# Main probabilities of a windowed attention turned as 64-row halves on TensorE, lower and upper queries into one PSUM bank each

## The reference, cut to what matters

```python
def light_attn(x, ln_g, ln_b, w_qkv, w_out):
    xn = layernorm(x, ln_g, ln_b)
    q, k, v = jnp.split(xn @ w_qkv, 3, axis=-1)
    q, k, v = (towin(q), towin(k), towin(v))
    kk, vv = (around(k), around(v))
    sim = jnp.einsum('bhnwd,bhnWd->bhnwW', q * DH ** (-0.5), kk)
    sim = jnp.where(kmask[None, None, :, None, :], sim, -jnp.finfo(sim.dtype).max)
    attn = jax.nn.softmax(sim, axis=-1)
    o = jnp.einsum('bhnwW,bhnWd->bhnwd', attn, vv)
    return o.transpose(0, 2, 3, 1, 4).reshape(b, n, HDH) @ w_out
```

## Time and profile before

| what | value |
|---|---|
| median of 3 executions | 4277.84 us (4275.5 to 4278.29) |
| the profiled execution's own time | 4279.63 us |
| its span, first to last instruction | 4277.9 us |
| mean granted TensorE clock | 0.968 |
| TensorE matmul busy | 3981.5 us (93%) |
| TensorE weight loads busy | 3281.4 us (77%) |
| VectorE busy | 2822.5 us (66%) |
| ScalarE busy | 1786.3 us (42%) |
| GpSimd busy | 876.8 us (20%) |

### The profile page before, as it was taken

The page is one execution under the profiler, slowest core; times in us unless marked ns, Lnnn a source line. Parts: engine busy times, 40 slices in busy tenths (PEclk is TensorE's granted clock), DMA queues, the critical chain, the costliest instruction groups (busy, mean ns, idle before and its releaser), DMA issues. The chain is left out here.

```text
span 4277.9 us, 96936 instructions
## 1 busy us (share of the span) xinstructions
PE 3981.5 (93%) x39328; PEld 3281.4 (77%) x39328; DVE 2822.5 (66%) x5012; ACT 1786.3 (42%) x4746; POOL 876.8 (20%) x663
## 2 busy tenths in 40 slices
PE   6788779999999999989999999968999999999998
PEld 5677767888888888878888888857777677777776
DVE  9888857776767676665555567574745646646546
ACT  7434323444444344434444433332544544534434
POOL 0222202222222322222222222221111011111011
PEclk9899979999999999999999999987999999999999
DMA  9688852322222232212221212122022022122021
GB/s 318 168 227 220 225 163 72 92 86 83 85 92 83 83 94 82 86 57 63 60 61 60 60 60 61 54 88 60 7 55 58 9 55 48 19 53 51 16 45 14
DMA packets 341371, 360.91 MB, mean 84 GB/s; under 512 B 23104, under 2 KB 237376, under 8 KB 340928
## 3 DMA queue, kind: packets, MB, share of 16 engines
q1 hardware_dynamic: 262592, 287.52, 22.7%
q0 software_dynamic: 12288, 33.56, 3.8%
q10 hardware_dynamic: 66048, 33.56, 2.9%
HBM read 228.21 MB, written 76.02 MB: 71 GB/s over the span
## 5 line engine op out<-in xcount | busy, mean ns | idle before, releaser
L1684 POOL TENSOR_TENSOR l_prob<-l_prob,l_inv 128x768 f32<-128x768 f32 x256 | 389.8, 1544 | 1690.9 <-DVE l_inv L1641 1690.9
L1235 ACT ACTIVATE l_prob<-l_ps_s,l_neg_max 128x192 f32<-128x192 f32 x1024 | 420.7, 443 | 7.6 <-DVE l_neg_max L1617 7.4
L2244 ACT ACTIVATE h_prob<-h_ps_s,h_neg_max 128x1024 f32<-128x1024 f32 x256 | 285.6, 1116 | 253.6 <-DVE h_neg_max L2318 253.6
L1617 DVE TENSOR_REDUCE l_neg_max<-l_ps_s 128x4 f32<-128x768 f32 x256 | 233.1, 952 | 237.4 <-PE l_ps_s L1004 218.4
L2315 DVE TENSOR_REDUCE h_neg_max<-h_ps_s 128x1 f32<-128x1024 f32 x256 | 312.4, 1221 | 50.9 <-PE h_ps_s L2103 42.6
L2372 DVE COPY h_probs_t<-h_ps_t 128x512 f32<-128x512 f32 x256 | 176.5, 690 | 180.4 <-PE h_ps_t L2117 180.1
L2134 PEld LDWEIGHTS h_ps_o<-h_probs_t,ahead_then_values 128*64 128x64 f32 x4096 | 223.8, 138 | 45.4 <-issue 45.4
L2134 PE MATMUL h_ps_o<-h_probs_t,ahead_then_values 128*64 128x128 f32 x4096 | 254.9, 278 | 0.0
L2117 PEld LDWEIGHTS h_ps_t<-ident,h_prob 64*128 64x128 f32 x4096 | 151.6, 140 | 112.0 <-issue 66.2
L1235 ACT ACTIVATION_READ_ACCUMULATOR l_prob<-l_ps_s,l_neg_max 128x1 f32 x1024 | 235.5, 230 | 0.0
L1004 PEld LDWEIGHTS l_ps_s<-l_k_t,l_q_t 64*64 64x64 f32 x6144 | 187.9, 132 | 48.1 <-issue 44.8
(11 more groups left out here) (413 smaller groups left out, 10800.0 us busy)
## 6 DMA issues: line engine op xcount, KB each, us to landing
toep_back<-taps_padded ACTq DMA_DIRECT2D x32, 1024.0 KB, 11.1
x<-xg SPq DMA_DIRECT2D x64, 512.0 KB, 9.1
l_xin<-x SPq DMA_DIRECT2D x128, 256.0 KB, 3.3
l_xres<-x SPq DMA_DIRECT2D x128, 256.0 KB, 3.2
l_val_side<-l_val SPq DMA_DIRECT2D x256, 128.0 KB, 3.1
out_dram<-l_res SPq DMA_DIRECT2D x128, 256.0 KB, 2.0
ahead_then_values<-x SPq DMA_DIRECT2D x126, 256.0 KB, 3.1
xin<-in_L_attn_x_dram SPq DMA_DIRECT2D x32, 768.0 KB, 6.4
```

Of the source, the lines that this page charges most:

```text
L1235: last = nc.scalar.activation(prob[t % 2][:, h, pair, :], ps_s[:, h, pair, BOTH], ACT.Exp, bias=neg_max[:, t % 2, h, pair:pair + 1], accum ...
L1617: nc.vector.tensor_reduce(neg_max[:, t % 2, h, :], ps_s[:, h, :, BOTH], AX_X, ALU.max, negate=True).then_inc(max_made, 1)
L1684: nc.gpsimd.tensor_tensor(mine, mine, spread(inv[:, t % 2, h, :], [1, PAIRS], [0, WIN + P]), ALU.mult).then_inc(p_normed, 1)
L2244: nc.scalar.activation(prob[i % 2][:, :].rearrange("p (a k) -> p a k", a=2), ps_s[i % 2][:, :, :], ACT.Exp, bias=neg_max[:, qt % 2, h:h + ...
```

## The change

Each transpose of 128 queries by 128 keys becomes two of 64 queries by 128 keys, one in the lower and one in the upper 64 rows of the array. The lower 64 queries of all eight heads go to `ps_b`, the upper ones to `ps_a`, so that VectorE and ScalarE each copy one half of the queries of every head instead of all queries of one half of the heads. As both banks are now written from the first pair on, the waits for `u1_kept` and `u2_kept` stand ahead of `turn_side`.

```diff
-                def turn_main(bank, j, h, made):
-                    for pair in range(PAIRS):
-                        last = nc.tensor.transpose(bank[:, pair * P:(pair + 1) * P], prob[j % 2][:, h, pair, MAIN],
-                                                   ident[:, :])
-                    last.then_inc(made, 1)
+                def turn_main(j):
+
+                    for n in range(HEADS):
+                        for rows, bank, made in ((LO, ps_b, main0_made), (HI, ps_a, main1_made)):
+                            last = nc.tensor.transpose(bank[:, n * WIN:(n + 1) * WIN],
+                                                       prob[j % 2][rows, n // PAIRS, n % PAIRS, MAIN], ident[rows, rows])
+                            if n == HEADS - 1:
+                                last.then_inc(made, 1)
...
                         wait(pe, p_normed, 2 * (g - 7))
+                        wait(pe, u1_kept, done(g - 3))
+                        wait(pe, u2_kept, done(g - 2))
                         wait(pe, res_made, g - 9)
                         turn_side(t)
-                        wait(pe, u1_kept, done(g - 3))
-                        turn_main(ps_b, t, 0, main0_made)
-                        wait(pe, u2_kept, done(g - 2))
-                        turn_main(ps_a, t, 1, main1_made)
+                        turn_main(t)
...
-                        nc.scalar.activation(pt_main[:, 1, :, :].rearrange("p a q -> p (a q)"), ps_a[:, :],
+                        nc.scalar.activation(pt_main[:, :, :, HI], ps_a[:, :].rearrange("p (h a q) -> p h a q", h=2, q=WIN),
...
-                        nc.vector.tensor_copy(pt_main[:, 0, :, :].rearrange("p a q -> p (a q)"),
-                                              ps_b[:, :]).then_inc(main0_kept, 1)
+                        nc.vector.tensor_copy(pt_main[:, :, :, LO],
+                                              ps_b[:, :].rearrange("p (h a q) -> p h a q", h=2, q=WIN)).then_inc(main0_kept, 1)
```

## The result

The changed kernel takes 4295.04 us (median of 7 runs, 4292.45 to 4297.32) against 4277.84 us for the kernel before, run beside it (7 runs too): a ratio of 1.0033 with a 95% interval of 1.0021 to 1.0045. It is slower, by 0.33%. The forecast was 4286 us, with 4270 to 4300 as its range and "slower by over 0.2%" as the likeliest of the three. The profiled execution has a span of 4294.0 us against 4277.9, so 16.1 us are to be accounted for, where the prediction's sum had 7.9. The median, 9 us above the point forecast, lies in the stated range but outside the 4280 to 4293 that the prediction gave its likeliest case.

A forecast was written before the change was run, and what follows sets the result against it. The prediction took TensorE's own queue to set the time in the light stage. From 4279.63 us profiled, a 30.7 us loss less a 22.8 us gain gave 4287.5, or 4286 us as median, range 4270 to 4300.

The forecast's parts named there:

- the prediction's sum: Whole kernel: loss of 30.7 us less gain of 22.8 us, so 7.9 us more.
- its likeliest case: Whole kernel: gain and loss both as costed, 4280 to 4293 us, chance 0.73.
- The turn: Light stage, end of turn_side to third unit's first matmul: 1.07 us instead of 1.26, 0.19 us gained in 120 steps.
- The rival in which the projection follows the new transposes as cheaply as the old: Projection behind the transposes: change of form free, gain 0.39 us a step, 4262 us in all; chance 0.08.
- the one in which the turn gains nothing: Rival at the transposes: drains on both sides eat the gain, the loss stands alone, 4309 us; chance 0.07.
- The moved wait: Steps with j % 4 == 2: turn_side waits for VectorE's keep of the query unit, 0.99 us lost in 31 steps.
- the rival of the lost clock: Matmuls behind the new waits run slow, 0.63 us instead of 0.40: 86 us more, 4371 us; chance 0.03.
- at_lo and the copies: Beside the third unit: VectorE's at_lo stays 0.13 us ahead of its matmul; copies of 64 columns in 128 cost nothing.

The follow-up runs named there:

- after_again: The changed kernel unaltered, run once more in a later series against the kernel before: 4289.11 us, ratio 1.0029.
- after_third: The changed kernel unaltered, run again beside its version with shifted code: 4293.26 us, ratio 1.0033 to the kernel before.
- after_shifted: The changed kernel plus 16 unused transposes where TensorE idles ahead of the routed loop: 4287.4 us, ratio 1.0019 to the kernel before.
- late_waits: The changed kernel with the waits for u1_kept and u2_kept ahead of the last head of turn_side: 4265.45 us, ratio 0.9976 to the kernel before.
- carrier: The changed kernel with both waits behind turn_side, on one extra 64-column matmul into ps_b: 4289.4 us, ratio 1.0012 to the kernel before.
- carrier_shifted: The changed kernel, both waits behind turn_side on one extra matmul, plus 16 unused transposes ahead of the light stage: 4273.54 us, ratio 0.9981 to the kernel before.

## Why the prediction was right, and what it lacked

**The turn: right.** 0.64 us for the transposes and 0.43 for the projection behind them were both taken from the heavy stage, and came out as 0.64 and 0.43 (1506.49 - 1506.06). From end to end the gain is 1.26 - 1.07 = 0.19 us, as predicted; measured over whole steps it is 16.92 - 16.75 = 0.17. The rival in which the projection follows the new transposes as cheaply as the old is out, and so is the one in which the turn gains nothing.

The Trainium skill, "TensorEngine Tiling (Array Packing)", Theoretical Speedup, states up to 2x for rows of at most 64. The runs show 1.03 / 0.64 = 1.6x for the turn alone, 1.26 / 1.07 = 1.2x with the projection behind it, and 1.03 / 0.94 = 1.1x when the halves don't alternate.

**The moved wait: right.** 31 waits, at the steps named, released when VectorE's keep of the query unit ends; turn_side's end comes 1.25 us behind that (1521.86 to 1523.11), against 1.30 in the sum. A step with the wait and the one behind it take 17.64 + 16.78 - 2 x 16.75 = 0.92 us more, against 0.99. The prediction was some 8% too high in this term and some 12% in the gain; over four steps these cancel: 0.92 - 4 x 0.17 = +0.24 us measured, 0.99 - 4 x 0.19 = +0.23 predicted. Moving the waits alone gave 30.45 us against 30.7. The next matmuls stay at 0.39 us, so the rival of the lost clock is out for these waits.

**at_lo and the copies: right.** at_lo ends 0.13 us ahead of the matmul that needs it, to the hundredth what was forecast, and does not bite in ordinary steps. The copies cost what they did (618 and 692 ns).

**What the sum lacked.** It had no term for the turns of loops; the stretch of the earlier trace rows ends at 1900 us, ahead of this one. The changed kernel's code lies otherwise, and at the turn of its routed loop TensorE waits 2.9 us more and loses 2.5 more in slow matmuls, 5.4 us in all. Undone by a shift of the code, it gave back 5.9 us, and the rest was 8.4 against the 7.9 predicted. That the position of the code decides was shown, by three pairs of kernels and a control; that the wait is for instructions is argued from the packets, as no view shows addresses or a releaser. The Trainium skill, "Advanced Engine Details and Errata", ISA Cache, says that instructions are held in lines of 16 KB, 256 of them to a line. The packets on q8 are of that size (322 for 5.28 MB), so the trace agrees; how far the 16 transposes moved the loop against a line isn't shown by any row. The sum also lacked the 2.6 us that the moved waits give back in step 2.

**What was luck.** The sum gave 7.9 us and 17.2 were measured; that 4295 us still lies in the range is owed to the room left on that side for a turn that gains nothing, which did not happen. And the sum lay on the edge between no change and slower: with the turn of the loop undone the ratio is 1.0019 (1.001 to 1.0028), just within 0.2%, so the side "slower" may well have been decided by something that the prediction didn't know of.

**Still open.** Why the clock falls in the last steps of one execution and not of another. The kernel unaltered came out between 9.8 and 17.2 us slower in three series, whose runs spread by 5 to 21 us. The traces show one source of this: the turns of the unrouted loop take 18.5 to 19.2 us as a rule, but 20.5 to 20.8 in one or two turns of after_again, after_third, after_shifted and late_waits, where matmuls take 0.63 us for a while after an idle stretch of 1.8 to 2.1 us.

**The version that beats both.** With the waits ahead of the last head of turn_side, the change is worth 0.24% (4265.45 us, ratio 0.9976), and 0.32% with the shifted code (0.9968), which can't be told from it. The plan of turning halves was sound; what made it slower was where its two waits stood, and to a lesser part the turn of the loop.

## What to carry to other kernels

When an edit joins two groups whose output goes to different buffers, their waits move ahead of both: look first for which buffer comes free last, and keep independent work of the engine between its release and its use. A wait that was hidden by 0.2 us cost 0.9 us when it was moved past a group of 1.1 us, five times what the faster group won. And where a difference of a few tenths of a per cent is to be explained or forecast, compare the steps at the turns of loops apart from the others: a few instructions more or less anywhere ahead of a loop can move its start to where a turn costs 4.5 to 5.5 us more, as here, which has nothing to do with the idea that is being tested; a shifted control kernel tells it. A single profiled execution of the kernel before can also be a lucky one in a stretch where the clock may fall: the last three steps of ours were, by 4 to 5 us.

## What the runs showed of the hardware

A program's own position made some 13 us of its time: carrier and carrier_shifted differ in 16 transposes in an idle stretch, and have ratios of 1.0012 and 0.9981 to the kernel before (4289.4 and 4273.54 us). Sixteen transposes added ahead of a loop made two kernels of four faster and the other two no slower.

Transposes of 64 rows that alternate between lower and upper rows start in pairs every 0.06 us (from 1505.46 to 1505.83 us seven into ps_b, six intervals); with all lower rows first the whole turn takes 0.30 us more. One matmul of the form 128*64, put between the last of turn_side and the transposes of 64*128, costs 0.12 us, twice the 0.06 us at which its like follow each other within turn_side. The Trainium skill, "TensorEngine Tiling (Array Packing)", Key Properties, says that changing the mode drains the engine; the 0.15 us between the last start of turn_side and the first transpose, against 0.06 within either group, agrees with it.

An idle stretch can be cheaper in two pieces than in one: where TensorE waited 1.72 and then 1.54 us with work between (step 2, changed kernel) it kept a granted clock of 1.00, and where it waited 2.77 us at once (kernel before) the step's mean fell to 0.85 and the step took 2.6 us longer.
